# Writing a convolution's silu with tanh, and letting expert steps run over an iteration's end

## What is computed

```python
xz = x_normed @ in_proj_w.T                      # x_ssm and z, 512 channels each
acc = causal convolution of x_ssm, 4 taps per channel
x_conv = silu(acc + conv_b)                      # silu(v) = v * sigmoid(v)
B, C, d = split(x_conv @ x_proj_w.T, 16, 16, 1)
delta = softplus(d)
h = exp(delta * A) * h + delta * B * x_conv      # per channel, 16 states, token after token
y = (sum over states of h * C + D * x_conv) * silu(z)
x = x + y @ out_proj_w.T
x = x + sum over the 2 best of 8 experts of weight * (layernorm(x) @ expert_w)
```

## Time and profile before

| | |
|---|---|
| median of 3 runs | 2886.32 us (2884.05 to 2886.54) |
| profiled execution, its own time | 2881.56 us |
| span of the profiled execution | 2879.6 us |
| TensorE busy | 2370.9 us, 82% |
| VectorE busy | 2256.9 us, 78% |
| GpSimd busy | 1811.0 us, 63% |
| ScalarE busy | 1489.0 us, 52% |
| granted TensorE clock, mean | 0.896 of full speed |

### The profile page before, as it was taken

How to read it: one execution, slowest core, us unless ns; L and a number is a source line. 1 busy time by engine, 2 the same in 40 slices (tenths; PEclk the granted TensorE clock), 3 DMA queues, 4 the chain that set the end, 5 groups by cost and what they waited for, 6 DMA issues and landing times.

```text
span 2879.6 us, 34506 instructions
## 1 busy us (share of the span) xinstructions
PE 2370.9 (82%) x9510; PEld 1385.9 (48%) x9510; DVE 2256.9 (78%) x3144; ACT 1489.0 (52%) x2417; POOL 1811.0 (63%) x1418
## 2 busy tenths in 40 slices
PE   5668777797988989797988989798897979798886
PEld 2335344454545455454545555454555545454433
DVE  3889898898888879898888879898888978877300
ACT  3454555465564646465464656555564646534221
POOL 2455666556565867667675766767686766757532
PEclk8777777798999989898998989899998989899998
...
GB/s 126 252 252 90 127 81 47 86 79 116 81 114 100 139 121 111 117 114 136 110 144 102 126 116 114 125 117 148 89 135 121 110 124 115 124 128 179 217 195 160
DMA packets 192570, 366.27 MB, mean 127 GB/s; under 512 B 22912, under 2 KB 22912, under 8 KB 192384
## 3 DMA queue, kind: packets, MB, share of 16 engines
...
## 4 chain that ended last, share of the span: by engine, by line
PE 39%; DVE 23%; issue 17%; POOL 9%; ACT 9%; DMA 2%; DVEq 0%; SPq 0%; POOLq 0%; ACTq 0%
PE work L1168 27%; DVE h L1002 10%; DVE acc L1010 9%; PE hT L1173 6%; POOL u L717 6%; PE work L1173 3%; ACT decay L863 3%; DVE xc L1033 2%; PE work L1228 2%; ACT L863 1%; POOL x_out L817 1%; ACT xc L915 1%; ACT acc L872 1%; DMA row_scratch<-x_first,row_at 1%; DMA b_ring<-b_scratch 1%
## 5 line engine op out<-in xcount | busy, mean ns | idle before, releaser
L717 POOL TENSOR_TENSOR u<-xc,b_ring 128x1024 f32<-128x1024 f32 x512 | 1228.7, 2404 | 770.5 <-DVE h L1002 587.5
L863 ACT ACTIVATE decay<-dt,neg_a 128x512 f32<-128x512 f32 x1024 | 699.6, 689 | 646.3 <-DVE h L1002 643.2
L1173 PE MATMUL hT<-ident,h 128*128 128x128 f32 x4096 | 697.7, 305 | 392.7 <-DVE acc L1010 316.6
L1173 PEld LDWEIGHTS hT<-ident,h 128*128 128x128 f32 x4096 | 527.0, 156 | 683.6 <-DVE acc L1010 332.2
L1002 DVE TENSOR_TENSOR_SCAN h<-decay,h_last,u 128x512 f32<-128x512 f32 x512 | 651.4, 1274 | 135.1 <-ACT decay L863 70.6
L1002 DVE TENSOR_TENSOR_SCAN h<-decay,u 128x512 f32<-128x512 f32 x512 | 620.1, 1213 | 162.1 <-ACT decay L863 97.4
L1010 DVE SCALAR_TENSOR_TENSOR acc<-hT,ct,acc 128x512 f32<-128x512 f32 x960 | 697.8, 727 | 59.2 <-PE hT L1173 58.6
L1168 PE MATMUL work<-w_exp,xeT 128*128 x1528 | 709.8, 608 | 31.0 <-issue 14.9
L1168 PE MATMUL work<-xnT,w_in 128*128 128x512 f32 x1024 | 486.5, 621 | 0.7 <-issue 0.7
L1168 PEld LDWEIGHTS work<-w_exp,xeT 128*128 128x128 f32 x1528 | 280.5, 193 | 342.9 <-issue 341.8
L1168 PEld LDWEIGHTS work<-xnT,w_in 128*128 128x128 f32 x1024 | 196.2, 202 | 203.8 <-issue 203.8
...
## 6 DMA issues: line engine op xcount, KB each, us to landing
...
```

Of the source, the lines that this page charges most:

```text
L717: nc.gpsimd.tensor_tensor(out=u[:, at:at + 2, :], in0=xc[:, half, 2 * k:2 * k + 2, :], in1=b_ring[:, n % ROWS:n % ROWS + 1, :].to_broadcas ...
L863: nc.scalar.activation(decay_bank[g % 2][:], dt[:, half, :], ACT.Exp, scale=neg_a[:, c, n:n + 1]).then_inc(decay_ready, 1)
L1173: last = nc.tensor.transpose(ps[:, k * P:(k + 1) * P], tile(k), ident[:])
```

## The change

**Silu of the convolution.** silu(v) = v/2 * (1 + tanh(v/2)). The convolution's weights and bias are halved once at the start (`halved`), so that the convolution gives v/2; its bias is now added in its first instruction (`conv_first`, Identity in place of Copy). Per chunk ScalarE computes the tanh into a side tile (`x_tanh`), `sp` for chunks 0 and 2 and `x_first` for 1 and 3, and VectorE multiplies (`x_gate`): (tanh + 1) * xc. Chunks 2 and 3 wait for the products of 0 and 1, since they share the side tiles; chunk 0 waits for the store of the B rows from `sp`, chunk 1 for the scatters from `x_first`, and the next `weigh`, which writes `x_first`, waits for the products.

**Expert steps.** Places of expert steps may be over 64: such a step is put into the next iteration, at its place less 64. Tiles are numbered through the whole kernel, and steps of one kind stay in the order of the tiles.

**Tables.** All tables of places have new numbers.

```diff
     COMBINE = {
-        "gather": [19.21, 20.41, 33.06, 35.43, 48.33, 52.85, 53.39, 61.42],
+        "gather": [10.32, 12.7, 30.15, 32.27, 40.21, 48.08, 51.15, 59.42],
...
     PREP = {
-        "silu_x": [38.14],
+        "x_tanh": [36.9, 36.95, 38.53, 39.02],
+        "x_gate": [36.58, 36.77, 38.02, 38.65],
...
     EXPERTS = {
-        "expert": [12.95, 13.84, 18.76, 27.8, 33.76, 34.9, 40.91, 47.46, 52.88, 56.98, 59.44, 64.58],
-        "expert_evict": [14.9, 16.13, 23.63, 35.21, 37.04, 39.9, 46.28, 54.52, 60.49, 62.6, 66.9, 66.9],
+        "expert": [13.06, 15.2, 19.47, 27.11, 33.46, 36.42, 40.91, 47.2, 52.02, 58.29, 62.83, 64.38],
+        "expert_evict": [17.31, 17.85, 23.7, 34.73, 37.76, 40.25, 48, 51.87, 57.7, 62.94, 65.09, 68.21],
...
+    def tile_places(j):
+        if j not in EXPERT_PLAN or j > BLOCKS:
+            return []
+        g, lo, count = EXPERT_PLAN[j]
+        table = {BLOCKS - 1: EXPERTS_LATE, BLOCKS: EXPERTS_END}.get(j, EXPERTS)
+        return [(kind if table is EXPERTS else kind.split("_", 1)[1], FIRST_TILE[g] + lo + i, at)
+                for kind, places in table.items() for i, at in enumerate(places) if i < count]
+
     def experts_in(j):
...
+        spots = {}
+        for of in (j - 1, j):
+            for kind, tile, at in tile_places(of):
+                if j == of + (at >= N * C and of < BLOCKS):
+                    spots.setdefault(kind, []).append((at - N * C * (j - of), tile))
+        return [(at, (kind, tile)) for kind, some in spots.items()
+                for at, tile in zip(sorted(at for at, _ in some), sorted(tile for _, tile in some))]
...
+                            nc.scalar.activation(w_conv[:], w_conv[:], ACT.Copy, scale=0.5).then_inc(halved, 1)
+                            nc.scalar.activation(b_conv[:], b_conv[:], ACT.Copy, scale=0.5).then_inc(halved, 1)
+                            act.wait_ge(halved, 2)
...
-                        last = nc.scalar.activation(xc[:, 1 - half, c, :], ps[:], ACT.Copy, scale=w_conv[:, c, EDGE:TAPS])
+                        last = nc.scalar.activation(xc[:, 1 - half, c, :], ps[:], ACT.Identity, bias=b_conv[:, c:c + 1], scale=w_conv[:, c, EDGE:TAPS])
...
-                    elif s[0] == "silu_x":
-                        for c in range(C):
-                            wait_used(act, j, ("project", c))
-                            if c == 0 and half == 0:
+                    elif s[0] == "x_tanh":
+                        c = s[1]
+                        wait_used(act, j, ("project", c))
+                        if c == 0:
+                            if half == 0:
                                 act.wait_ge(edge_added, j // 2 + 1)
-                            nc.scalar.activation(xc[:, 1 - half, c, :], xc[:, 1 - half, c, :], ACT.Silu, bias=b_conv[:, c:c + 1]).then_inc(xc_ready, 1)
+                            wait(act, b_stored, 16 * p)
+                        elif c == 1:
+                            wait(act, first_scattered, 16 * Q * (j - 1))
+                        else:
+                            act.wait_ge(xc_ready, p * C + c - 1)
+                        nc.scalar.activation(x_side_of(c)[:], xc[:, 1 - half, c, :], ACT.Tanh).then_inc(x_tanh, 1)
...
+                    elif s[0] == "x_gate":
+                        c = s[1]
+                        dve.wait_ge(x_tanh, p * C + c + 1)
+                        nc.vector.scalar_tensor_tensor(out=xc[:, 1 - half, c, :], in0=x_side_of(c)[:], scalar=1.0, in1=xc[:, 1 - half, c, :],
+                                                       op0=ALU.add, op1=ALU.mult).then_inc(xc_ready, 1)
...
+                            act.wait_ge(xc_ready, min(p + 1, BLOCKS) * C)
```

236 lines of the change are left out of this document (118 added, 118 removed).

## The result

The changed kernel takes 2935.2 us (median of 4 runs, 2928.36 to 2940.32) where the kernel before took 2886.43 us in the same comparison: ratio 1.0165, 95% interval 1.0139 to 1.0191, so 48 us slower. The prediction said 2834 us with a range up to 2874, and 0.87 for faster. It was wrong in its direction.

A forecast was written before the change was run, and what follows sets the result against it. No engine is busy throughout; VectorE, which owns the scan, waits for decays and `u`. Terms -36.6 - 3.6 - 4 - 8 = -52 us from 2881.6 give 2829, and 4.8 us for the median gives 2834, range 2795 to 2874.

The forecast's parts named there:

- The boundary: Between iterations, moved expert steps shorten VectorE's first decay wait: 36.6 us saved behind odd iterations, 3.6 behind even ones.
- the transpose of `h` that VectorE needs in its fourth sum: On TensorE behind the moved last expert product after the boundary: just fits, or 0 to 1.2 us are lost.
- the wait at the boundary moves on: Rival: the stretch after the boundary, at a low clock, ends later; 22 to 44 us return, 2856 to 2878; chance 0.14.
- Silu as tanh: In 16 blocks, VectorE's added products take the place of its waits and ScalarE saves 32 table loads: together -4 us.
- The bound of +47: Upper bound for the tanh split: none of VectorE's waits go, so its added products cost 47 us in all.
- The other tables: New places elsewhere: a first-quarter wait goes, but a gather precedes the last `y_gate`; taken as 0, between -25 and +25 us.
- the wait of 4.47 us: In the first quarter, from a transpose's eviction behind an output projection, which stands elsewhere in the new order.
- The later waits for `u`: VectorE's waits of 1.76 and 1.25 us, two gathers now spread: -8 us over twelve iterations, between -30 and +10.
- The tail: Iterations 15 to 18: one expert tile moves from 15 into 16, TensorE's products unchanged; 0, plus or minus 8 us.
- The collision rival: New VectorE products block with GpSimd's `u` on shared SBUF ports: up to 150 us, slower 0.07; mild, +20 to +35, 0.13.

The follow-up runs named there:

- f3_front_back: The changed kernel with the first half of an iteration, the last eviction and iteration 15's tile table at the old places: 2892.99 us, ratio 1.0027.
- h2_front19: The changed kernel with the steps up to place 18, the last eviction and iteration 15's tile table back at old places: 2918.24 us, ratio 1.0101.
- h1_front14: The changed kernel with only the steps up to place 13 back at old places, last eviction at 67.9: 2921.34 us, ratio 1.0116.
- f4_fall_gathers: e3_fall_only with the sixth and seventh gather moved apart, from 52.85 and 53.39 to 51.2 and 56.9: 2866.60 us, ratio 0.9935.
- g1_tanh_ahead: The kernel before with the tanh split alone, all four tanh and products ahead of the scan at place 38: 2957.23 us, ratio 1.0245.
- j1_rows_evict_first: h2_front19 with ScalarE's eviction of the third tile's transposed rows moved from 20.34 to 19.1, ahead of the second norm2 eviction: 2878.81 us, ratio 0.9976.
- e3_fall_only: The kernel before with only the last two expert steps of each kind at the changed kernel's places, silu in one pass: 2871.18 us, ratio 0.9927.
- i1_fall_late_evict: e3_fall_only with its last two expert evictions at 66.1 and 67.9 instead of 65.09 and 67.0: 2868.31 us, ratio 0.9926.

## Why the prediction was wrong

Four differences of ratios account for the result. Fall-through: 1 to 0.9927, -21 us. The second half's new places, with silu: 0.9927 to 0.9993, +19 us, the collision of `picked_row` with `u` among them. The tanh split: 0.9993 to 1.0027, +10 us. The first half's new places: 1.0027 to 1.0165, +40 us. Together +48 us. The late iterations' tables are counted with the halves; they were not separated. Such a sum depends on its order: fall-through and the split have other prices at other places.

- **The boundary, -40 us forecast.** The wait behaves as the prediction put it, 7.39 to 1.58 us, and 2.12 to 1.80 behind even iterations. The gain of 36.6 us behind odd iterations came too: 6.1 us at the last four places, six times. The term is mis-sized by what comes back, and 21 us are left of it. The prediction followed the last product and allowed 0 to 1.2 us of loss at "the transpose of `h` that VectorE needs in its fourth sum". It didn't look at the product ahead of it, moved to 62.83, which took 5.39 us, and 2.6 us were lost at the second sum and the third scan. The rival "the wait at the boundary moves on" (22 to 44 us come back) was near in its number, 19 did, and in the lower clock, but it too had the other product.
- **Silu as tanh, -4 us forecast.** The instructions came as predicted (65 loads, products of 0.68 us with nothing in front of them). The split costs 10 us in two surroundings, with the collision of `picked_row` in both differences; waits and saved table loads, which were to pay for the 44 us of products, so paid for some three quarters of them. The bound of +47 held in this order only: at the old places the split costs 70 to 85 us, since it lengthens the chain from x to the next decays and collides with `u`.
- **The other tables: "I take 0, between -25 and +25".** This is the step that failed. Every place is new, but the term prices the first quarter only, by one wait of 4.47 us and a guess, and the sum has none for the second quarter, which it so put at nothing without a reason. The first quarter behaved: the wait of 4.47 us went, and places 4 to 15 are 3.2 us shorter in even iterations and 1.6 in odd ones. The second quarter, places 16 to 31, is 6.9 us longer on average in both kinds, and f3_front_back, with the old places there, is 40 us faster. TensorE was busy 40.68 of 43.35 us in that stretch at a granted clock of 1.00, so a gap of TensorE finds little room there: in h2_front19 a gap of 1.98 us and a product slower by 1.70 us cost 3.32 us of the window. That gap is shown to come from an order on ScalarE, where the expert rows' eviction stands behind `norm2`'s, and reversing it gives 36 us. In the changed kernel the product is as slow, but TensorE's gap ahead of it, 1.51 us, waits for VectorE. Which of the new places make that gap stays open; h1_front14 takes 14 us of the 40 away by places up to 13 and leaves the gap.
- **The later waits for `u`, -8 us forecast.** They went, and f4_fall_gathers shows that spreading gathers is worth nothing: the next `u` is late instead.
- **The tail, 0.** 0.1 us shorter from the last scan on; iteration 15, counted in it, is 2.4 us shorter.
- **The collision rival** had the right mechanism, with both of its signs seen in g1_tanh_ahead (products over 1.5 us, a longer `u`), but looked for it only at the new products, where it struck in g1_tanh_ahead and not in the changed kernel. The order showed `row_of` beside the moved `u`; `picked_row` was not priced because it took 0.19 us before.

What stays open: which steps up to place 13 cost their 0.5%, what makes TensorE's gap in the changed kernel, the product ahead of the transposes at the boundary, what the collision costs with the cast counted, and how much a kernel with j1_rows_evict_first's order, silu in one step and ranked rows in PSUM would give; by the differences above (10 and 7 us) some 17 us more, an estimate and not a run. The fastest kernels run are e3_fall_only, f4_fall_gathers and i1_fall_late_evict, 19 to 21 us under the kernel before and not told apart.
